# A transformer block on one Trainium2 core: the negated score maxima reach the second score product by 32x32 turns on VectorE and small DMAs, no longer by eight more TensorE transposes a tile

## The reference, cut to what matters

```
h = ln(x, ln1);  q, k, v = h @ wq + bq, h @ wk + bk, h @ wv + bv     # q scaled by 1/4
q, k = rope(q), rope(k)
a = softmax(q @ k.T, causal=True) @ v                # per head, 16 heads of 16
x = x + a @ wo + bo
h = ln(x, ln2);  q from h, k and v from the context ctx              # no mask
x = x + softmax(q @ k.T) @ v @ wo + bo
x = x + gelu(ln(x, ln3) @ fc1 + b1) @ fc2 + b2
s = softmax(x @ ctx.T);  t = s @ ctx
out = tanh(concat(x, t) @ trans_W + trans_b) + x
```

## Time and profile before

| | |
|---|---|
| median of 3 runs | 3378.58 us (3377.08 to 3378.83) |
| profiled execution | 3377.42 us; its span, from first to last instruction, 3375.6 us |
| busy: TensorE / VectorE / ScalarE / GpSimd | 96% / 72% / 66% / 43% |
| mean granted TensorE clock | 0.985 |
| DMA | 22 GB/s over the span |

### The profile page before, as it was taken

The page is one execution under the profiler, slowest core; times in us unless marked ns, Lnnn a source line. Parts: engine busy times, 40 slices in busy tenths (PEclk is TensorE's granted clock), DMA queues, the critical chain, the costliest instruction groups (busy, mean ns, idle before and its releaser), DMA issues.

```text
span 3375.6 us, 98793 instructions
## 1 busy us (share of the span) xinstructions
PE 3233.6 (96%) x40908; PEld 2750.2 (81%) x40908; DVE 2440.5 (72%) x5068; ACT 2211.2 (66%) x4737; POOL 1447.4 (43%) x2180
## 2 busy tenths in 40 slices
PE   3799999999999999999999999999999999999997
PEld 2588888888888888888888888888888888888886
DVE  3577777777777777777777777777777777777773
ACT  0367667666666666676676676666666766766764
POOL 0344444444444444444444444444444444444431
PEclk7799999999999999999999999999999999999998
DMA  3000000000000000000000000000000000000000
GB/s 89 20 16 21 27 20 21 27 20 22 25 21 26 21 21 27 21 21 27 20 21 27 21 21 27 20 25 22 21 27 21 21 27 21 20 27 21 21 13 10
DMA packets 83132, 79.62 MB, mean 24 GB/s; under 512 B 11904, under 2 KB 82432, under 8 KB 82688
## 3 DMA queue, kind: packets, MB, share of 16 engines
q1 hardware_dynamic: 82688, 73.30, 7.3%
HBM read 56.49 MB, written 16.78 MB: 22 GB/s over the span
## 4 chain that ended last, share of the span: by engine, by line
PE 86%; DVE 5%; POOL 4%; issue 3%; SPq 0%; ACT 0%; DMA 0%; DVEq 0%; POOLq 0%; ACTq 0%
PE sc L396 13%; PE A L365 12%; PE B L370 8%; PE B L372 6%; PE B L371 6%; PE B L444 4%; POOL kcf L1144 4%; PE C L370 3%; PE A L370 3%; PE C L371 3%; PE A L371 3%; PE C L372 3%; PE A L372 3%; PE A L455 3%; PE A L583 3%; PE B L365 3%
## 5 line engine op out<-in xcount | busy, mean ns | idle before, releaser
L1144 POOL TENSOR_TENSOR kcf<-tkc,rope_c 128x256 f32<-128x256 f32 x128 | 125.0, 976 | 671.5 <-DVE tkc L737 671.5
L750 DVE TENSOR_REDUCE qkz<-sc 128x8 f32<-128x1024 f32 x256 | 301.7, 1220 | 51.0 <-PE sc L386 51.0
L1008 ACT ACTIVATE pt_s<-sc 128x512 f32<-128x512 f32 x512 | 264.4, 602 | 105.2 <-PE sc L386 105.2
L750 DVE TENSOR_REDUCE qcz<-sc 128x8 f32<-128x1024 f32 x256 | 300.4, 1216 | 0.0
L1008 ACT ACTIVATE pt_c<-sc 128x512 f32<-128x512 f32 x512 | 264.5, 604 | 7.4 <-PE sc L396 5.9
L1149 POOL TENSOR_TENSOR rstd<-bmv,eps_t 128x1 f32<-128x1 f32 x384 | 84.0, 219 | 429.8 <-DVE bmv L720 429.8
L1144 POOL TENSOR_TENSOR qkf<-tqk,rope_c 128x512 f32<-128x512 f32 x128 | 211.6, 1653 | 121.2 <-DVE tqk L734 121.2
L365 PE MATMUL A<-ident,qkz 128*128 128x128 f32 x1536 | 240.8, 280 | 15.2 <-DVE qkz L794 7.9
L1151 POOL TENSOR_TENSOR rstd<-rstd,mhalf 128x1 f32<-128x1 f32 x384 | 234.4, 610 | 30.1
L974 ACT COPY kt_c<-A 128x512 f32<-128x512 f32 x128 | 75.1, 587 | 245.5 <-PE A L365 245.5
L1144 POOL TENSOR_TENSOR qcf<-tqc,rope_c 128x256 f32<-128x256 f32 x128 | 93.3, 729 | 324.7 <-DVE tqc L734 324.7
(11 more groups left out here) (230 smaller groups left out, 11532.7 us busy)
## 6 DMA issues: line engine op xcount, KB each, us to landing
rows_in<-in_x SPq DMA_DIRECT2D x128, 128.0 KB, 2.2
xt_f<-in_x_t SPq DMA_DIRECT2D x128, 128.0 KB, 2.2
rows_in<-in_ctx_t SPq DMA_DIRECT2D x128, 128.0 KB, 2.3
out<-o_out SPq DMA_DIRECT2D x128, 128.0 KB, 1.7
pt_s<-in_L_xattn_fc_w SPq DMA_DIRECT2D x1, 1024.0 KB, 5.0
rows_in<-in_L_xattn_fc_w SPq DMA_DIRECT2D x1, 1024.0 KB, 5.4
w_out_s<-in_L_xattn_sa_wo SPq DMA_DIRECT2D x4, 64.0 KB, 5.5
w_out_c<-in_L_xattn_ca_wo SPq DMA_DIRECT2D x4, 64.0 KB, 4.2
```

The source lines that it names most:

```text
L750: dve.tensor_reduce(out, sc[:, 2 * h:2 * h + 2, :].rearrange("p r (g k) -> p r g k", g=G), AX_X, ALU.max, negate=True).then_inc(signal, 1)
L1008: act.activation(pt[c][:, r, :, :].rearrange("p g q -> p (g q)"), sc[:, r, :], ACT.Exp).then_inc(signal, 1)
L1144: pool.tensor_tensor(out[:, :].rearrange("p (h e) -> p h e", e=HD), t[:, :].rearrange("p (h e) -> p h e", e=HD), rope_c[:, :].unsqueeze(1) ...
```

## The change

The second transposition on TensorE is dropped. ScalarE copies the bank of the first transposition twice, once to `qt` and once to `qtm`, now a ring of two; its row `MX` is then overwritten. VectorE writes the negated maxima into a small tile `z` (128x4x32, zero elsewhere), turns its 32x32 blocks into `zt` (a new instruction after each pair of reductions), and SyncE carries the rows to `qtm` by four DMAs for each tile and attention, each of four partitions with 128 numbers in pieces of 32. `p2s` and `p2c` wait for these DMAs. The names `after`, `n`, `U` and the loop pairs `(i, u)` become plain tile numbers, and waits that another wait already implies are left out; the order of the other steps and their banks stay.

```
+        qtm = {c: ring(f"qtm_{c}", [P, G, P], 2) for c in "sc"}
+        z, zt = [{c: sb(f"{name}_{c}", [P, G, 32]) for c in "sc"} for name in ("z", "zt")]
 # SyncE
+            def max_rows(c, t, landed):
+                for i in range(G):
+                    sp.dma_start(qtm[c][t % 2][MX:P:32, :, 32 * i:32 * i + 32],
+                                 zt[c][32 * i:32 * i + G, :, :]).then_inc(landed[t % 2], 16)
+            def zd_s_(t):
+                if live(t):
+                    need(sp, s["zt_s"], done(t))
+                    max_rows("s", t, zd_s)
+            def slot(u):
+                zd_s_(u - 3)
+                ld_x_(u)
+                ld_t_(u - 1)
+                ld_c_(u - 2)
+                store_(u - 9)
+                zd_c_(u - 4)
 # TensorE
-            def trqm_s(at):
-                if live(at):
-                    after(at, (("tqk", 1, 2),), (("ghib", 1, -3),))
-                    transposes(A0, qz["s"].rearrange("p h e -> p (h e)"), G).then_inc(s["trqm_s"], 1)
-            def trqm_c(at):
-                if live(at):
-                    pe.wait_ge(s["max_c"], 2 * n(at))
-                    after(at, (("fexp", 1, -3),), (("h3_lo", 1, 0),), (("kt_s", 1, 3),))
-                    transposes(A1, qcz[:, :, :].rearrange("p h e -> p (h e)"), G).then_inc(s["trqm_c"], 1)
+            def p2s_(t):
+                if live(t):
+                    need(pe, zd_s[t % 2], 64 * (t // 2 + 1))
+                    heads(kt["s"][t % NB["kt_s"]], qtm["s"][t % 2], 2 * HD, False)
+                    diagonal_mask(mask_t_bf).then_inc(s["p2s"], 1)
+            def p2c_(t):
+                if live(t):
+                    need(pe, zd_c[t % 2], 64 * (t // 2 + 1))
+                    need(pe, s["max_s"], 2 * done(t + 2))
+                    heads(kt["c"][t % NB["kt_c"]], qtm["c"][t % 2], 2 * HD, True).then_inc(s["p2c"], 1)
+            def trf_(t):
+                if live(t):
+                    need(pe, s["qtm_c"], done(t + 4))
+                    if t % 2 == 0:
+                        need(pe, s["x3"], done(t))
+                    transposes(B0, x3[t % R][:, :], KC).then_inc(s["trf"], 1)
+            def y_c_(t):
+                    need(pe, s["norm_c"], done(t))
+                    need(pe, s["qtm_s"], done(t + 3))
+            def f1a_(t):
+                    need(pe, s["tqc"], done(t + 2))
 # VectorE
             def maxima(c, signal):
                 for h in range(2):
-                    out = qz[c].rearrange("p (g r) e -> p r g e", r=G)[:, 2 * h:2 * h + 2, :, MX]
+                    out = z[c][:, :, 0:G].rearrange("p g r -> p r g")[:, 2 * h:2 * h + 2, :]
                     dve.tensor_reduce(out, sc[:, 2 * h:2 * h + 2, :].rearrange("p r (g k) -> p r g k", g=G),
                                       AX_X, ALU.max, negate=True).then_inc(signal, 1)
+            def turned(c, signal):
+                dve.transpose(zt[c][:, :, :].rearrange("p g a -> p (g a)"),
+                              z[c][:, :, :].rearrange("p g b -> p (g b)")).then_inc(signal, 1)
 # VectorE, slot: max_s_(u-1), then zt_s_(u-1), st1_, mv1_ ...; at its end max_c_(u-2), zt_c_(u-2)
 # ScalarE
+            def qtm_s_(t):
+                if live(t):
+                    copy(qtm["s"][t % 2][:, :, :], per_k(A1, 2 * E), s["qtm_s"])
+            def qtm_c_(t):
+                if live(t):
+                    copy(qtm["c"][t % 2][:, :, :], per_k(B0, 2 * E), s["qtm_c"])
+# ScalarE, slot: ... ct_hi_, qt_s_(u), qtm_s_(u), exp_s_ ...; kt_s_(u), qt_c_(u-2), qtm_c_(u-2), h3_hi_, x3t_, x2t_hi_
```

More of the change, by code:

```diff
@@ L167, in build @@
         st_o = [sem(f"st_o{i}") for i in range(2)]
+        zd_s, zd_c = [[sem(f"zd_{c}{i}") for i in range(2)] for c in "sc"]
         names = ("st1", "mv1", "var1", "rstd1", "xt_hi", "xt_lo", "qk", "tqk", "vs", "v_s",
-                 "cosqk", "rotqk", "addqk", "trq_s", "qt_s", "trk_s", "kt_s", "p1s", "max_s", "trqm_s", "qtm_s",
+                 "cosqk", "rotqk", "addqk", "trq_s", "qt_s", "trk_s", "kt_s", "p1s", "max_s", "zt_s", "qtm_s",
                  "p2s", "exp_s", "pv_s", "ot_s", "rinv_s", "att_s", "norm_s", "xres_s", "y_s", "x1",
                  "st2", "mv2", "var2", "rstd2", "xres_c", "trx2", "x2t_hi", "x2t_lo", "qc", "tqc",
-                 "cosqc", "rotqc", "addqc", "trq_c", "qt_c", "p1c", "max_c", "trqm_c", "qtm_c",
+                 "cosqc", "rotqc", "addqc", "trq_c", "qt_c", "p1c", "max_c", "zt_c", "qtm_c",
                  "p2c", "exp_c", "pv_c", "ot_c", "rinv_c", "att_c", "norm_c", "y_c", "x2",
@@ L224, in build, with live, live_pair, steps @@
         N_CST = 16 * (1 + 8 + 5 + 6 + 1 + 10)
[L226 to L237, removed]
+        def live(t):
+            return 0 <= t < TILES
+        def live_pair(t):
+            return 1 <= t <= TILES
+        def steps(slot, extra):
+            for u in range(TILES + extra):
+                slot(u)
         block = ctx.enter_context(nc.Block())
@@ L290, in load_c @@
[L290 to L305, removed]
@@ L398, in heads, with qk_, vs_ @@
                 return mm
[L400 to L403, removed]
+            def qk_(t):
+                if live(t):
+                    need(pe, s["ghib"], pairs(t - 4))
+                    if t <= 4:
+                        need(pe, s["xt_lo"], done(t))
                     split3_k(A0[:, :], (xt_hi, xt_lo), "sqk").then_inc(s["qk"], 1)
-            def vs(at):
-                if live(at):
+            def vs_(t):
+                if live(t):
+                    if 2 <= t <= 5:
+                        need(pe, s["qtm_c"], done(t - 2))
@@ L408, in vs, with trq_s_ @@
                     split3_k(B0[:, 0:E], (xt_hi, xt_lo), "sv").then_inc(s["vs"], 1)
[L410 to L413, removed]
+            def trq_s_(t):
+                if live(t):
+                    need(pe, s["addqk"], done(t))
+                    need(pe, s["ftan"], done(t - 7))
@@ L456, in project, with y_s_ @@
                 mm.then_inc(s["y_" + c], 1)
[L458 to L466, removed]
-                    transposes(A0, x1[:, :], KC).then_inc(s["trx2"], 1)
[L469 to L472, removed]
+            def y_s_(t):
+                if live(t):
+                    need(pe, s["norm_s"], done(t))
+                    project("s", A0)
@@ L492, in p2c @@
[L492 to L496, removed]
-            def pv_c(at):
-                if live(at):
-                    after(at, (("cw", 1, 1),))
-                    pv("c", at, B0)
-            def y_c(at):
-                if live(at):
-                    after(at, (("qt_s", 1, 4),), (("ftan", 1, -3),))
-                    pe.wait_ge(s["norm_c"], n(at))
-                    project("c", at, A1)
@@ new lines, in qt_s_, with kt_s_ @@
+            def qt_s_(t):
+                if live(t):
+                    need(act, s["trq_s"], done(t))
+                    copy(qt["s"][:, :, :], per_k(A1, 2 * E), s["qt_s"])
+            def qtm_s_(t):
+                if live(t):
+                    copy(qtm["s"][t % 2][:, :, :], per_k(A1, 2 * E), s["qtm_s"])
+            def kt_s_(t):
+                if live(t):
+                    need(act, s["trk_s"], done(t))
+                    copy(kt["s"][t % NB["kt_s"]][:, :, :], per_k(A1, 2 * E), s["kt_s"])
@@ new lines, in v_s_, with exp_s_ @@
+            def v_s_(t):
+                if live(t):
+                    if t >= TILES - 1:
+                        need(act, s["vs"], done(t))
+                    act.activation(vaug["s"][t % NB["vaug_s"]][:, :, 0:HD],
+                                   B0[:, 0:E].rearrange("p (h e) -> p h e", e=HD), ACT.Copy, scale=rstd[0][:, 0:1]).then_inc(s["v_s"], 1)
+            def exp_s_(t):
+                if live(t):
+                    need(act, s["p2s"], done(t))
+                    exps("s", s["exp_s"])
```

1033 lines of the change are left out of this document (516 added, 517 removed).

## The result

The changed kernel takes 3337.14 us (median of 4 runs, 3335.67 to 3337.47), the kernel before 3378.12 us beside it (4 runs, 3377.08 to 3378.83). The ratio is 0.9878, with a 95% interval of 0.9861 to 0.9895: faster by 41 us. The forecast was 3362, a gain of 16. The direction was right and the time lies in the whole range, 3330 to 3405, but the gain is two and a half times the one forecast, and the time lies outside the forecast's own range of 3345 to 3375.

The account below looks back on a forecast made before the run. TensorE's in-order work was taken as the bound. Per slot -0.22 (f1a) -0.43 (trqm_s) +0.48 (trf) = -0.17 us, -21 us over 124 slots, +5 at the ends: -16, so 3362 us; own range 3345 to 3375 (50%), whole range 3330 to 3405.

Parts of the forecast that it names:

- The waits that the diff drops: Waits removed by the diff: put at zero, at most 0.12 us behind an ACT release, once a slot.
- f1a: TensorE without trqm_c ahead of f1a: f1a's load, held by tqc, gains 0.22 of the 0.39 us a slot.
- trq_s: TensorE turn needing addqk: expected to start at 1521.95, with addqk done by 1521.4.
- trqm_s: Turn removed from TensorE between f2a and pv_c: saves 0.43 us a slot, bounds 0.33 and 0.53.
- trf: TensorE load waits for ACT copy qtm_c instead of qt_c: loses 0.48 us a slot, bounds 0 and 0.6.
- rival B: At trf, ACT's copies or the order make the 0.48 loss vanish: -0.65 us a slot, about 3302 us; 9%.
- addqk and trq_s: VectorE's addqk no longer waits for trqm_s: done by 1521.4, before trq_s starts on TensorE at 1521.95.
- f2a and hla: zt_s delays tqk by 0.34 us; hla ends at 1518.97, f2a wants it by 1519.1: 0.1 us of slack.
- rival C: Gain used up at hla's slack or by zt_c's 0.45 at f1a: no change, about 3378 us; 19%.
- The DMAs: Row copies before p2c: land 2.2 us after issue, hidden with 0.37 us to spare.
- Rival A: Late DMA landing holds p2c: at 2.8 us from issue, 0.35 us a slot, about 3405 us; 22%.
- The ends: First and last slots, where less work covers the new latency: together +5 us.

Follow-up runs that it names:

- edit 2: Changed kernel with a satisfied wait put back ahead of the late one at qc, trx3, trf and addkc: 3361.88 us, period 24.97.
- edit 1: Kernel before with only the order of waits changed, the late one first at qc, trx3, trf and addkc: 3360.97 us, ratio 0.9942.
- edit 5: Changed kernel with ScalarE's qt_c and qtm_c moved behind kt_c, ahead of xhat and kt_s: 3275.15 us, ratio 0.9688.
- edit 10: Changed kernel with its cross-attention part undone and ScalarE's qt_c moved behind kt_c: 3304.26 us, ratio 0.9777.
- Edit 6: Changed kernel with GpSimd's fout (o_out) moved behind kr_s, away from addqk: 3320.97 us, ratio 0.9834.
- edit 9: Changed kernel with two more DMAs of four partitions and 2 KB ahead of qtm_c's four: 3411.7 us, ratio 1.0095.
- first half alone: Changed kernel with the cross-attention part undone (trqm_c back on TensorE) and the self-attention part kept: 3300.87 us, ratio 0.9769.
- its second: The cross-attention part; run alone, as the changed kernel with trqm_s back on TensorE behind f2a: 3376.06 us, ratio 0.9991.
- edits 1 and 8: For 8: changed kernel with qc, trx3 and trf waiting for two semaphores in every slot, the late one first: 3336.12 us, ratio 0.9874.

## Why the forecast was right in its direction and wrong in its size

The step that failed is this one: "The waits that the diff drops I put at zero: matmuls with and without one follow at the same spacing; the most they could give is the 0.12 us behind an ACT release, once a slot." Its first half looked at waits that are satisfied when the instruction comes up; p1c, which lost one of its two, starts no earlier for it (+0.03 in the table). But the diff also left the late wait first, or alone, at four places where another had stood ahead of it: qc, trx3, trf and addkc. There the instruction starts 0.03 to 0.06 us behind its releaser's end, not 0.10 to 0.12. Three places that count (trx3's is hidden behind trf's), and not one, give 0.20 us a slot (24.97 against 24.77), 25 us (edit 2), or 19 (edit 1, where trx2 holds part of it back). With them the forecast would have been 3337 to 3343; that it would then have met the time is partly luck, since two further errors, at f1a and at trq_s, nearly cancel.

By its own steps, per slot:

- f1a: gain forecast 0.22, measured 0.36 (mis-sized). zt_c's 0.31 us was right; xt_lo overlaps it, so tqc ends 0.05 us earlier than forecast, and the load follows tqc by 0.05, not 0.11. The 0.11 was taken from trf, where two waits stood; f1a's load has one in both kernels.
- trqm_s: 0.43 forecast, 0.44 measured. Right.
- trf: 0.48 forecast, 0.47 from trx3 to trf measured; edit 5 takes 0.50 us a slot back. Right, and rival B (the loss is covered) is out. The gap of 0.28 that stood there before, which the prediction held against B, was itself worth nothing (edit 10): x1 let trx2 start no earlier.
- addqk and trq_s: "it is done by 1521.4, trq_s starts at 1521.95" failed. Freed of its wait for trqm_s, addqk moves beside o_out and takes 1.04 us, and rs_qk ahead of it beside qkf takes 0.87: counted from p1s, addqk ends at 9.75 us and not at 9.28, and holds trq_s by 0.10 to 0.12. Edit 6 shows it at 0.10 us a slot, some 12 of its 16 us; the rest is in the first and last slots. This error hid the one at f1a.
- f2a and hla: the 0.1 us of slack held; f2a moves with f1a and rival C's price is not paid.
- The DMAs: hidden, as forecast, with 0.55 to spare and not 0.37 (edit 9). Rival A is out by that much. Two errors met here: the issues stand 0.58 us apart and not 0.5, the last 0.24 later for it, and the landing is 0.6 us shorter than the 2.2 taken.
- The ends: +5 forecast, +4 measured.

The terms: -0.17 forecast, -0.14 at f1a, -0.20 at the waits, +0.11 at trq_s make -0.40; measured -0.36. The 0.04 that is left are steps of 0.01 to 0.03 at places that nothing in the study singles out.

## What to carry to other kernels

Where an instruction of a bounding engine waits for several semaphores, write the wait for the one that comes last first: 0.06 to 0.07 us a release here, 19 and 25 us for four places in 128 slots with no work changed. When a wait is taken from an instruction, look at what the other engine runs where it now lands, not only at when it can start. And a change in two halves should be run in halves: this one's first half alone was worth 79 us, some 20 of them by the order of the waits, and its second was worth 26 to 29 us only when its added copy was moved off the path.

## What the runs showed of the hardware that was not expected

The cost of a satisfied wait ahead of the late one appears on TensorE behind ScalarE (0.12 against 0.06 us) and on VectorE behind GpSimd. For addkc, the kernel before and the changed one:

```profile
1526.70 0.97 POOL L1144 TENSOR_TENSOR kcf<-tkc,rope_c 128x256 f32<-128x256 f32 x1 [5.23 <-DVE tkc L737]
1527.77 0.43 DVE L931 TENSOR_TENSOR kcz<-kcf,rs_kc 128x256 f32<-128x256 f32 x1 [0.22 <-POOL kcf L1144]
```

```profile
1508.12 0.98 POOL L1167 TENSOR_TENSOR kcf<-tkc,rope_c 128x256 f32<-128x256 f32 x1 [4.70 <-DVE tkc L703]
1509.13 0.43 DVE L703 TENSOR_TENSOR kcz<-kcf,rs_kc 128x256 f32<-128x256 f32 x1 [0.23 <-POOL kcf L1167]
```

kcz starts 0.10 us behind kcf's end in the first and 0.03 in the second. A copy of four partitions from SBUF to SBUF, 2 KB in pieces of 128 B, lands in about 1.6 us, with 0.57 us of issue time; it is no slower to land than the stores of 128 KB (1.7).

Why a wait's place matters, the packed traces show in records that the timeline leaves out (before trf it says `issue`). Of the waits ahead of an instruction, the first one written is carried by the instruction itself; a further one is a semaphore instruction of its own ahead of it, 0.051 us long on TensorE and 0.021 on VectorE. In the kernel before, trf's load carries x3, and qt_c has the extra instruction: it starts at 1507.20, 0.04 behind the end of qt_c, is over at 1507.26, and the load starts at 1507.28. In edit 1 the load itself carries qt_c, and starts 0.05 behind its end. The extra instruction costs when it is the one that is released last, and in edits 1 and 8, where it was done before, it costs nothing. It also explains trx2 in edit 1: both of its waits are for the same count of x1, so one of them is an extra instruction released last, whatever the order; the load starts 0.12 behind x1, and 0.05 in edits 5 and 10, where there is one wait. The changed kernel still has such places: addqk waits for cosqk and then for rotqk, and starts 0.10 behind the end of rs_qk, where zt_c, with one wait, starts 0.03 behind max_c. No run reorders those.
